# Silu taken by ScalarE's own function in two groups a tile, z kept raw and projected one tile ahead

## The chip, the cores and the metric

The kernel runs as one program on 1 core of one Trainium2 chip. The metric is the device time of that core in microseconds (us), shown as the median of several executions. The engines are called PE (TensorE, the matmuls), ACT (ScalarE), DVE (VectorE), POOL (GpSimd) and SP (SyncE, which here only issues DMAs). They run in parallel, each works off its own list of instructions in order, and they wait for each other through semaphores.

## The reference, cut to what matters

64 images of 37 tokens (36 patches and a class token) and 256 features go through an embedding, a state-space mixer, a layer norm, a mixture of experts (32 experts, 8 chosen for a row, and one shared expert) and a second layer norm. All values are float32. `_silu(v)` is `v * sigmoid(v)`. It stands in four places:

```python
x_d, z = jnp.split(xz, 2, axis=-1)
...
x_d = _silu(jnp.moveaxis(xc + conv_b[None, :, None], 1, 2))
...
delta = jax.nn.softplus(dt_raw * W_dt[:, 0] + b_dt)
...
h = dA * h + d_t[..., None] * b_t[:, None, :] * u_t[..., None]
y = jnp.einsum('bds,bs->bd', h, c_t)
...
y = jnp.moveaxis(ys, 0, 1) + D_param * x_d
y = y * _silu(z)
...
h = jax.nn.silu(flat @ wg.T) * (flat @ wu.T)
...
shared = jax.nn.silu(flat @ shared_gate_w.T) * (flat @ shared_up_w.T) @ shared_down_w.T
```

The recurrence over `h` has 16 states for each of 512 inner features, and softplus needs a logarithm and an exponential.

## The kernel before, in words

**Tiles and slots.** The images are cut into 11 tiles, the first of 4 images (148 columns) and ten of 6 (222 columns). The 512 inner features lie on 128 partitions in 4 pieces, so a full buffer of a tile is 128x888 and half of one 128x444. The first part of the program is one loop over tiles `i` and 16 slots `s`; slot `s` is also the state of the recurrence, and `g = 16 * i + s`. Every engine runs this loop by itself, in an order that the code writes out. While tile `i` does its recurrence, the slots also carry the front of tile `n = i + 1` (embedding, projection, convolution, silu, softplus) and the back of tile `t = i - 1` (gate, output projection, norm, router, shared expert), which `pieces(i, s)` of each engine places.

**One state of the recurrence.** ACT makes the decay factors, four activations for a state (`decays`, L1118: two for each of the PSUM banks D0 and D1). PE spreads the rows of B and C over the partitions into the bank BC (`spread`, L824); the bank for one state may be written once the read of the state two before is done. ACT copies B to SBUF (`copy_b`, L1106). POOL multiplies it with `du`, which is the drive (`drives`, L630), two states ahead; the drive of slot 0 is made by DVE itself (L1395). DVE scans both halves (`scan`, L1408, twice) and multiplies with C (`reads`, L1420). PE adds up the reads over the states (`add_up`, L842). A bank D can be filled for the next state only when the scan has used it.

**POOL's other work.** From tile 2 on POOL issues 16 scatters a tile (L618, rows of the tile two before, to DRAM). It also holds the expert allocation of the tile (L570 to L607, small operations in slots 12, 14 and 15), the norm's root (L413 to L418), and in slot 14 one product for softplus (L637, 128x888). DVE needs that product for `delta` (L1382) and then makes `du` (L1387), and the next tile's decays and drives need those.

**Silu before.** Silu is computed as x * (1 + tanh(x / 2)), with a factor of one half moved into later operations. ACT evaluates tanh from the PSUM bank and DVE finishes with one operation: for the convolution in slots 1 and 8 of ACT (L1056) and slots 2 and 9 of DVE (L1354), for z in slots 12 and 14 of ACT (L1062) and 13 and 15 of DVE (L1426), and for the shared expert from slot 7 (L1158, L1462).
**After the loop** follow the experts: 179 blocks of 128 rows. For each block PE turns the rows (L1001), multiplies with gate and up (L1007), turns the hidden values (L1013) and multiplies with the down weights (L1021), each step one block behind the one before it. POOL gathers the results and DVE adds them up.

## Time and profile before

| what | us |
|---|---|
| median of 3 runs | 1134.51 |
| lowest, highest | 1130.51, 1134.89 |
| the profiled execution | 1135.04 |
| its span in the trace | 1133.2 |
| DVE busy | 928.9 |
| PE busy | 964.0 |
| POOL busy | 788.1 |
| ACT busy | 681.6 |

The span is the time from the first to the last instruction in the trace; 1.8 us of the profiled execution lie around it. Busy times are sums over the whole span, and the parts have different limits: up to about 94 us the first tiles are filled in, up to about 772 us the loop over tiles runs, and from about 819 us the experts. A row of a timeline gives the start in us from the span's start, the length in us, the engine and the line of the kernel; in square brackets stands how long the engine was idle before it and what ended that.

### The profile page before, as it was taken

The page shows a single profiled execution, that of the slowest core. Times are in us where ns is not written, and L with a number is a line of the kernel's source. Part 1 is how long each engine was busy: PE and PEld are TensorE (multiplying, and loading weights), DVE is VectorE, ACT ScalarE, POOL GpSimd, SP SyncE. Part 2 cuts the span into 40 slices and gives each one's busy share as a digit, 9 for nine tenths or more (in the row PEclk, how much of TensorE's full clock was granted, in tenths as well). Part 3 has the DMA queues.
Part 4 walks back from the last instruction along what each step waited for, and adds up shares of the span by engine and source line. Part 5 has one row for each costly group of instructions (what it writes and reads, how often), then busy time and mean ns, then how long its engine had stood idle before and what let it go on. Part 6 is the DMA issues. An engine that isn't in the chain of part 4 may idle for free.

```text
span 1133.2 us, 16674 instructions
## 1 busy us (share of the span) xinstructions
PE 964.0 (85%) x4563; PEld 725.6 (64%) x4563; DVE 928.9 (82%) x1821; ACT 681.6 (60%) x1802; POOL 788.1 (70%) x839
## 2 busy tenths in 40 slices
PE   5698889988798888989978896866599999999990
PEld 5575666656566566666756663534388888878880
DVE  3589999999999999999999999896244677767774
ACT  3685675757567575666757657541266666666661
POOL 2244478878788787888878888787501676767775
PEclk8999999999999999999999999878799999999996
DMA  4599500201111020111202010058566898889883
GB/s 150 176 327 325 160 24 24 62 15 59 38 50 52 19 80 18 54 42 33 74 15 59 10 53 29 28 210 354 146 188 179 251 269 263 260 259 277 265 265 108
DMA packets 104474, 149.21 MB, mean 132 GB/s; under 512 B 14111, under 2 KB 91359, under 8 KB 104127
## 3 DMA queue, kind: packets, MB, share of 16 engines
q1 hardware_dynamic: 87487, 106.35, 29.3%
q0 software_dynamic: 16896, 41.80, 13.0%
q8 instruction: 38, 0.62, 0.2%
q14 instruction: 53, 0.43, 0.1%
HBM read 71.28 MB, written 76.82 MB: 131 GB/s over the span
## 4 chain that ended last, share of the span: by engine, by line
POOL 26%; PE 26%; issue 18%; DVE 17%; ACT 7%; DMA 3%; SPq 1%; POOLq 0%; DVEq 0%; ACTq 0%
POOL arena L630 11%; PE BC L1007 11%; DVE arena L1408 9%; POOL pool_dram L618 6%; PE Y L1001 3%; PE F L1021 3%; PE K L1021 3%; DMA mixer_own<-pool_dram 3%; DVE arena L1420 2%; ACT D L1118 2%; PE Y L842 2%; POOL arena L637 1%; PE D L1013 1%; ACT arena L1069 1%; POOL gat L686 1%
## 5 line engine op out<-in xcount | busy, mean ns | idle before, releaser
L1408 DVE TENSOR_TENSOR_SCAN arena<-D,arena 128x444 f32<-128x444 f32 (+1 forms) x352 | 351.1, 1037 | 12.4 <-ACT D L1118 8.3
L842 PE MATMUL Y<-arena,ident 128*128 128x444 f32 (+1 forms) x704 | 303.3, 559 | 1.6 <-DVE arena L1420 1.6
L686 POOL DMA_INDIRECT gat<-y_dram,slot_all x176 | 173.5, 986 | 127.5 <-DMA y_dram<-mixer_own 72.5
L618 POOL DMA_INDIRECT pool_dram<-hrow,slot_of x176 | 175.4, 997 | 45.3 <-issue 38.1
L630 POOL TENSOR_TENSOR arena<-mixer_own,arena 128x888 f32<-128x888 f32 (+1 forms) x90 | 163.9, 1823 | 53.2 <-ACT arena L1106 51.6
L1118 ACT ACTIVATE D<-mixer_own,aneg 128x216 f32<-128x216 f32 (+1 forms) x384 | 148.5, 427 | 82.4 <-DVE arena L1408 82.2
L1420 DVE TENSOR_TENSOR arena<-arena,BC 128x888 f32<-128x888 f32 (+1 forms) x176 | 184.8, 1050 | 5.4
L1007 PE MATMUL BC<-arena,xt 128*128 x716 | 185.3, 382 | 0.0
L630 POOL TENSOR_TENSOR arena<-arena 128x888 f32<-128x888 f32 x75 | 143.4, 1913 | 53.8 <-ACT arena L1106 52.9
L842 PEld LDWEIGHTS Y<-arena,ident 128*128 128x128 f32 x704 | 127.0, 199 | 74.8 <-issue 70.0
L1118 ACT ACTIVATE D<-arena,aneg 128x216 f32<-128x216 f32 x320 | 126.8, 437 | 73.1 <-DVE arena L1408 73.1
L1672 DVE SCALAR_TENSOR_TENSOR act_g<-tanh_g,BC 128x128 f32<-128x128 f32 x179 | 51.5, 288 | 106.4 <-ACT tanh_g L1259 103.9
L824 PE MATMUL BC<-bc_rows,sel 96*128 96x222 bf16 (+1 forms) x352 | 62.8, 260 | 85.9 <-DVE arena L1420 85.9
L1007 PEld LDWEIGHTS BC<-arena,xt 128*128 128x128 f32 x716 | 123.0, 192 | 9.5 <-issue 0.3
L824 PEld LDWEIGHTS BC<-bc_rows,sel 96*128 96x128 bf16 x352 | 29.4, 98 | 122.2 <-DVE arena L1420 109.5
L1106 ACT ACTIVATE arena<-BC 128x222 f32<-128x222 f32 (+1 forms) x165 | 56.4, 342 | 57.7 <-PE BC L824 57.7
L765 PEld LDWEIGHTS F<-arena 128*128 128x128 f32 x352 | 68.2, 208 | 22.0 <-issue 13.0
L1001 PE MATMUL Y<-ident,mixer_own 128*128 128x128 f32 x358 | 70.0, 278 | 11.2 <-DMA mixer_own<-pool_dram 10.8
L765 PE MATMUL F<-arena 128*128 128x210 f32 (+7 forms) x352 | 76.0, 364 | 4.0 <-DVE arena L1322 1.9
L1255 ACT ACTIVATE xt<-Y 128x256 f32<-128x256 f32 x179 | 67.2, 376 | 18.3 <-PE Y L1001 18.3
L1259 ACT ACTIVATE tanh_g<-BC 128x128 f32<-128x128 f32 x179 | 49.5, 277 | 43.1 <-PE BC L1007 43.1
L735 PE MATMUL F<-arena 128*128 128x216 f32 (+1 forms) x264 | 54.8, 364 | 21.8 <-ACT mixer_own L1070 8.7
(232 smaller groups left out, 1644.1 us busy)
## 6 DMA issues: line engine op xcount, KB each, us to landing
mixer_own<-pool_dram SPq DMA_DIRECT2D x179, 144.0 KB, 3.6
y_dram<-mixer_own SPq DMA_DIRECT2D x179, 128.0 KB
...
```

The lines of the kernel that those rows point to most:

```text
L618: nc.gpsimd.indirect_dma_start(out=pool_rows, out_offset=bass.IndirectOffsetOnAxis(ap=slot_of[q][0:r, b, k:k + 1], axis=0), in_=hrow[q][0: ...
L630: nc.gpsimd.tensor_tensor(cut(drive[g % DRIVES], i), cut(du[i % 2], i), b_row[pooled(g) % B_ROWS][:, None, 0:width(i)].broadcast_to([P, KI ...
L686: nc.gpsimd.indirect_dma_start(out=gat[0:r, k, b, :], out_offset=None, in_=y_rows[0:(blocks_by(t) - k) * P, :], in_offset=bass.IndirectOff ...
L765: nc.tensor.matmul(to.rearrange("p (a t) -> p a t", t=TOKENS)[:, :, back:], diag_w[:, c, TAPS - 1 - back, :], of[:, :, 0:TOKENS - back], s ...
L824: mm = nc.tensor.matmul(BC[g % 2][:, j * N:j * N + w], sel[:, STATES * j + s, :], bc_rows[i % 2][:, 0:w], start=True, stop=True)
L842: mm = nc.tensor.matmul(Y[j][:, 0:w], ident[:], read[g % 3][:, j * w:(j + 1) * w], start=(s == 0), stop=(s == STATES - 1), skip_group_chec ...
L1001: mm = nc.tensor.transpose(PX[b % 2][:, k * P:(k + 1) * P], xg[b % XG][:, k * P:(k + 1) * P], ident[:])
L1007: mm = nc.tensor.matmul(PG[b % 2][:, 0:DM], xt[b % 2][:, k * P:(k + 1) * P], weights[k], start=(k == 0), stop=(k == KM - 1))
L1021: nc.tensor.matmul(PY[b % 2][:, 0:DM], hidt[b % 2][:], weights, start=True, stop=True).then_inc(down_done, 1)
L1118: last = nc.scalar.activation(D[b][:, c * w:(c + 1) * w].rearrange("p (a t) -> p a t", t=TOKENS)[:, :, 1:TOKENS], cut(delta[i % 2], i)[:, ...
L1408: nc.vector.tensor_tensor_scan(state[g % 2][:, lo:hi], D[b][:, 0:hi - lo], drive[g % DRIVES][:, lo:hi], 0.0, ALU.mult, ALU.add).then_inc(s ...
L1420: nc.vector.tensor_tensor(cut(read[g % 3], i), cut(state[g % 2], i), BC[g % 2][:, None, N:N + width(i)].broadcast_to([P, KI, width(i)]), A ...
```

## The change

- ACT evaluates `Silu` itself in place of tanh, and DVE's finishing operations are gone. The factors of one half go too.
- `Silu` is in a set of its own, apart from Exp and Ln. The calls are therefore put in two groups a tile. Slot 1 holds the first half of the convolution. Slot 8 holds the shared expert's gate, the second half of the convolution and z. Behind each group the set with Exp and Ln is loaded again.
- z of tile n is projected in slots 12 and 14 of the tile before it (`project_z(n, b)` in place of `project_z(i, b)`), copied raw to SBUF by two ACT copies (`take_z`), and its silu is one operation from SBUF to SBUF (`silu_z`, 128x888) in slot 8 of the tile's own loop.
- DVE's `softplus_small` goes from slot 13 to 12, and `softplus_large` from behind the read of slot 13 to ahead of it. The shared expert's product goes from slot 8 to slot 9, between scan and read.
- In the experts, `hidden` has one DVE operation in place of two.

```diff
+            def silu_first(n):
+
+                act.wait_ge(conv_done, KI * n + 2)
+                if n > 1:
+                    act.wait_ge(x_added, n - 1)
+                    act.wait_ge(du_done, n - 1)
+                nc.scalar.activation(cut(x2[n % 2], n)[:, 0:2, :], pair(F, n), ACT.Silu).then_inc(x2_done, 1)
+                nc.scalar.preload_act_table_set("natural_log_exp_and_others")
+
+            def silu_second(n):
+                act.wait_ge(conv_done, KI * n + 4)
+                nc.scalar.activation(cut(x2[n % 2], n)[:, 2:4, :], pair(F, n), ACT.Silu).then_inc(x2_done, 1)
+
+            def take_z(n, b):
+                act.wait_ge(z_done, 2 * n + b + 1)
                 if n > 0:
...
+                    act.wait_ge(z2_done, n)
+                nc.scalar.activation(cut(z_raw, n)[:, 2 * b:2 * b + 2, :], pair(K, n), ACT.Copy).then_inc(z_taken, 1)
+
+            def silu_z(i):
+                act.wait_ge(z_taken, 2 * i + 2)
                 if i > 0:
...
+                    act.wait_ge(gated_done, 2 * i)
+                nc.scalar.activation(cut(z2, i), cut(z_raw, i), ACT.Silu).then_inc(z2_done, 1)
...
                 if front and s == 1:
-                    tanh_conv(n, 0)
+                    silu_first(n)
...
-                if back and s == (7 if mix else 9):
+                if back and s == (8 if mix else 9):
                     shared_gate(t)
                 if front and s == 8:
-                    tanh_conv(n, 1)
+                    silu_second(n)
+                if mix and s == 8:
+                    silu_z(i)
+                if mix and s == 8:
+                    nc.scalar.preload_act_table_set("natural_log_exp_and_others")
...
-                if mix and s in (12, 14):
-                    tanh_gate(i, (s - 12) // 2)
+                if front and s == 14:
+                    take_z(n, 1)
...
-                    nc.scalar.preload_act_table_set("natural_log_exp_and_others")
                     softplus_ln(n)
                     softplus_series(n)
+                    take_z(n, 0)
...
-                if front and s == 2:
-                    silu_conv(n, 0)
...
-                if front and s == 9:
-                    silu_conv(n, 1)
-                if back and mix and s == 8:
-                    shared_expert(t)
...
-                if mix and s in (13, 15):
-                    silu_z(i, (s - 13) // 2)
-                if front and s == 13:
-                    softplus_large(n)
...
+                    if 1 <= i < TILES and s == 9:
+                        shared_expert(i - 1)
                     if i + 1 < TILES and s == 12:
                         split(i + 1, 1)
+                        softplus_small(i + 1)
                     if i + 1 < TILES and s == 13:
-                        softplus_small(i + 1)
+                        softplus_large(i + 1)
...
             def hidden(b):
-                dve.wait_ge(g_tanh, b + 1)
-                nc.vector.scalar_tensor_tensor(act_g[b % 2][:], tanh_g[b % 2][:], 1.0, PG[b % 2][:, 0:HID], ALU.add,
-                                               ALU.mult).then_inc(g_act, 1)
...
+                dve.wait_ge(g_silu, b + 1)
+                nc.vector.tensor_tensor(hid[b % 2][:], silu_g[b % 2][:], PG[b % 2][:, HID:2 * HID], ALU.mult).then_inc(hid_done, 1)
```

ACT from slot 7 to slot 9 of tile 2, before. `ex` is the router's exponential, `D0` and `D1` take the decays, `BC` to arena is `copy_b`, `arena<-F` is the tanh of the convolution:

```order
L1149 ACTIVATE ex<-K 111x64
L1152 ACTIVATE ex<-ex,one_col 111x64
L1158 ACTIVATE tanh_s<-K 128x222
L1106 ACTIVATE arena<-BC1 128x222
L1118 ACTIVATE D0<-mixer_own,aneg 128x6x36 x2
L1118 ACTIVATE D1<-mixer_own,aneg 128x6x36 x2
L1056 ACTIVATE arena<-F 128x444
L1106 ACTIVATE arena<-BC0 128x222
L1118 ACTIVATE D0<-mixer_own,aneg 128x6x36 x2
L1118 ACTIVATE D1<-mixer_own,aneg 128x6x36 x2
```

The same stretch now, where L1119 is `copy_b` and L1131 the decays:

```order
L1162 ACTIVATE ex<-K 111x64
L1165 ACTIVATE ex<-ex,one_col 111x64
L1119 ACTIVATE arena<-BC1 128x222
L1131 ACTIVATE D0<-mixer_own,aneg 128x6x36 x2
L1131 ACTIVATE D1<-mixer_own,aneg 128x6x36 x2
L1171 ACT_TABLE_LOAD
L1171 ACTIVATE silu_s<-K 128x222
L1061 ACTIVATE arena<-F 128x444
L1073 ACTIVATE mixer_own<-mixer_own 128x888
L1224 ACT_TABLE_LOAD
L1119 ACTIVATE arena<-BC0 128x222
L1131 ACTIVATE D0<-mixer_own,aneg 128x6x36 x2
L1131 ACTIVATE D1<-mixer_own,aneg 128x6x36 x2
```

Between the decays of slot 8 and the `copy_b` of slot 9 stood one activation; now two table loads and three activations stand there.

ACT in slots 1 and 2 of tile 3, before and then now:

```order
L1179 ACTIVATE slot_all<-slot8 111x16
L1056 ACTIVATE arena<-F 128x444
L1118 ACTIVATE D0<-arena,aneg 128x6x36 x2
L1106 ACTIVATE arena<-BC1 128x222
L1118 ACTIVATE D1<-arena,aneg 128x6x36 x2
```

```order
L1192 ACTIVATE slot_all<-slot8 111x16
L1056 ACT_TABLE_LOAD
L1056 ACTIVATE arena<-F 128x444
L1057 ACT_TABLE_LOAD
L1131 ACTIVATE D0<-arena,aneg 128x6x36 x2
L1119 ACTIVATE arena<-BC1 128x222
L1131 ACTIVATE D1<-arena,aneg 128x6x36 x2
```

One table load stands ahead of the activation on F and one behind it, before the decays and the `copy_b` of slot 2.

DVE in slots 12 and 13, before. The first row is the pair of scans of slot 12, L1371 is `softplus_small`, L1426 the finishing of z, L1376 `softplus_large`:

```order
L1408 SCALAR_TENSOR_TENSOR arena<-D,arena 128x444 x2
L1366 TENSOR_TENSOR bc_rows<-rest,mid 32x222
L1420 TENSOR_TENSOR arena<-arena,BC 128x888
L1408 SCALAR_TENSOR_TENSOR arena<-D,arena 128x444 x2
L1371 TENSOR_SCALAR arena<-arena 128x888
L1420 TENSOR_TENSOR arena<-arena,BC 128x888
L1426 SCALAR_TENSOR_TENSOR mixer_own<-mixer_own,K 128x444
L1376 SCALAR_TENSOR_TENSOR arena<-arena,ln_small,mixer_own 128x888
```

And now, where L1418 is the scan and L1430 the read:

```order
L1418 SCALAR_TENSOR_TENSOR arena<-D,arena 128x444 x2
L1376 TENSOR_TENSOR bc_rows<-rest,mid 32x222
L1381 TENSOR_SCALAR arena<-arena 128x888
L1430 TENSOR_TENSOR arena<-arena,BC 128x888
L1418 SCALAR_TENSOR_TENSOR arena<-D,arena 128x444 x2
L1386 SCALAR_TENSOR_TENSOR arena<-arena,ln_small,mixer_own 128x888
L1430 TENSOR_TENSOR arena<-arena,BC 128x888
```

The finishing of z is gone, and the two softplus operations each stand ahead of a read.

## Rows read from the trace of the kernel before

**Rows 1.** Windows: core, busy us of each engine (instructions), TensorE's granted clock, DMA share, GB/s.
```profile
300.00:720.00 420.00, 362.01 (x1588) 257.90 (x1587) 405.44 (x583) 269.29 (x691) 347.07 (x358) 0.96 0.13 40
819.00:1100.00 281.00, 278.69 (x1526) 232.42 (x1527) 186.09 (x637) 179.75 (x524) 162.89 (x167) 1.00 0.84 248
```

**Rows 2.** Waits of DVE, 300 to 720 us: who, for whom, us, times, longest.
```profile
DVE arena L1408 <- POOL arena L630: 1.6, 6, 0.3
```

**Rows 3.** Waits of POOL, 100 to 720 us.
```profile
POOL arena L630 <- ACT arena L1106: 73.6, 63, 6.4
```

**Rows 4.** Groups of instructions on DVE: count, busy us, mean ns, idle before them.
```profile
L1672 DVE SCALAR_TENSOR_TENSOR act_g<-tanh_g,BC 128x128 f32<-128x128 f32 x179 | 51.5, 288 | 106.4 <-ACT tanh_g L1259 103.9 <-issue 1.0
...
L1354 DVE SCALAR_TENSOR_TENSOR arena<-arena,F 128x444 f32<-128x444 f32 (+1 forms) x22 | 13.1, 597 | 8.8 <-ACT arena L1056 8.8
L1426 DVE SCALAR_TENSOR_TENSOR mixer_own<-mixer_own,K 128x444 f32<-128x444 f32 (+1 forms) x22 | 13.1, 596 | 0.0
...
L1462 DVE SCALAR_TENSOR_TENSOR act_s<-tanh_s,K 128x222 f32<-128x222 f32 (+1 forms) x11 | 4.1, 373 | 0.0
```

**Rows 5.** Timeline of POOL: softplus products of tiles 1, 5, 6 and 9.
```profile
149.68 2.06 POOL L637 TENSOR_TENSOR arena<-arena 128x888 f32<-128x888 f32 x1 [1.08 <-DVE arena L1376]
...
424.92 2.08 POOL L637 TENSOR_TENSOR arena<-arena 128x888 f32<-128x888 f32 x1
...
492.87 2.09 POOL L637 TENSOR_TENSOR arena<-arena 128x888 f32<-128x888 f32 x1
...
696.94 2.08 POOL L637 TENSOR_TENSOR arena<-arena 128x888 f32<-128x888 f32 x1
```

**Rows 6.** Timeline of ACT: a table load and its neighbour, then a softplus exponential.
```profile
427.64 1.28 ACT L1062 ACT_TABLE_LOAD   x1
428.94 0.54 ACT L1062 ACTIVATE mixer_own<-K 128x444 f32<-128x444 f32 x1
...
482.72 0.94 ACT L1090 ACTIVATE arena<-arena 128x888 f32<-128x888 f32 x1
```

**Rows 7.** Timeline of POOL, tile 6: drives 4, 5, 11, 13 and 14.
```profile
444.10 1.91 POOL L630 TENSOR_TENSOR arena<-mixer_own,arena 128x888 f32<-128x888 f32 x1 [1.51 <-ACT arena L1106]
...
447.73 1.93 POOL L630 TENSOR_TENSOR arena<-mixer_own,arena 128x888 f32<-128x888 f32 x1 [0.50 <-ACT arena L1106]
...
469.03 1.92 POOL L630 TENSOR_TENSOR arena<-mixer_own,arena 128x888 f32<-128x888 f32 x1
...
479.38 1.93 POOL L630 TENSOR_TENSOR arena<-mixer_own,arena 128x888 f32<-128x888 f32 x1 [0.49 <-ACT arena L1106]
...
483.99 1.92 POOL L630 TENSOR_TENSOR arena<-mixer_own,arena 128x888 f32<-128x888 f32 x1 [0.31 <-ACT arena L1106]
```

**Rows 8.** Timeline of ACT, tile 6, slots 8 and 9: decays, then `copy_b`.
```profile
464.55 1.53 ACT L1118 ACTIVATE D<-mixer_own,aneg 128x216 f32<-128x216 f32 x4
...
467.19 0.35 ACT L1106 ACTIVATE arena<-BC 128x222 f32<-128x222 f32 x1
```

**Rows 9.** Timelines of DVE and POOL: operations beside one of the other engine.
```profile
467.78 0.17 DVE L1505 TENSOR_SCALAR gmask<-gleft 111x16 f32<-111x16 f32 x1
...
489.22 2.80 DVE L1376 SCALAR_TENSOR_TENSOR arena<-arena,ln_small 128x888 f32<-128x888 f32 x1 [0.36 <-ACT arena L1098]
...
491.23 1.63 POOL L618 DMA_INDIRECT pool_dram<-hrow,slot_of  x1 [0.17 <-issue]
...
742.13 1.91 POOL L630 TENSOR_TENSOR arena<-mixer_own,arena 128x888 f32<-128x888 f32 x1
...
742.52 1.56 DVE L1505 TENSOR_SCALAR gmask<-gleft 111x16 f32<-111x16 f32 x1
```

**Rows 10.** Timeline of DVE, tile 6: the router's weights (slot 10), then `delta` (slot 14).
```profile
476.66 0.28 DVE L1522 SCALAR_TENSOR_TENSOR wsel<-eleft,masked 111x64 f32<-111x64 f32 x1
...
495.76 1.14 DVE L1382 SCALAR_TENSOR_TENSOR arena<-arena,ln_small 128x888 f32<-128x888 f32 x1
```

**Rows 11.** The chain that ended last, fill-in of tile 0: start, us, what.
```profile
45.72 0.69 ACT D L1118 x2
```

108 lines of the change are left out of this document (41 added, 67 removed).

## The prediction

> **What bounds the kernel now.** I read the windows first, then the waits, then the timelines of one steady tile. The experts are PE's: in a window of 281.0 us PE is busy for 278.7 at a granted clock of 1.00, DVE for 186.1 [rows 1]. What DVE saves there gives nothing as long as PE stays full.
>
> The loop over tiles looks like DVE's, with 405.4 busy us of 420.0 [rows 1], and in that stretch its scans wait for POOL for only 1.6 us in all [rows 2]. But POOL is close behind. It issues sixteen scatters in each of tiles 2 to 9, and its idle time there is nearly all waits for `copy_b` on ACT [rows 3], in the slots from 1 to 4 and then in crumbs [rows 7]. A tile closes into a circle: POOL's softplus product (slot 14) ends, DVE makes `delta`, runs slots 15, 0 and 1, ACT copies B, POOL makes drive after drive and scatter after scatter up to the next product. The product starts at 149.68 in tile 1 and at 696.94 in tile 9 [rows 5], eight tiles later: 547.26 / 8 = 68.41 us a tile. In tile 6 the product ends at 492.87 + 2.09 = 494.96, and DVE takes it at 495.76 [rows 5, 10]. So POOL is only 0.8 us ahead of DVE in that circle. This is the number on which the forecast turns: DVE can come forward by 0.8 us and then waits for the product.
>
> **The change part by part.** DVE loses, for a tile, two finishing operations of the convolution and two of z at 0.60 each and one of 0.37 [rows 4]. Their overlap with the next operation is some 0.07, so they hold the queue for 4 x 0.53 + 0.3 = 2.4. The wait of 0.36 for the logarithm [rows 9] goes as well, since a table load no longer stands ahead of Ln. That is 2.8 us a tile off DVE. The product with the shared expert's up values stays, as do gate and `du`, with the same sizes.
>
> ACT gets four table loads a tile for two. A load takes 1.28, and the activation behind it starts 0.02 after its end: 427.64 + 1.28 = 428.92, then 428.94 [rows 6]. So I take 1.3 for a load with its surroundings.
>
> The Trainium skill, page "ScalarE: Activation LUTs", section "What ACT_TABLE_LOAD costs", says that a switch costs a drain of about 1.38 us beside the load. By that rule each group, with its two switches, would hold ACT for some 2.8 us more, which is an estimate from that page. The trace does not agree: no such gap stands behind the load.
>
> Slot 1: load 1.28, silu in the 0.54 of tanh (same shape, PSUM to SBUF), load 1.28: ACT is held for 3.1 us where it was held for 0.5. Queued behind are the decays of slot 3 and `copy_b` of drive 4. Slot 8: load 1.28, shared gate 0.3, convolution 0.5, z as one 128x888 operation at the 0.94 of the softplus exponential [rows 6], load 1.28: 4.3 less overlaps, 4.2. Queued behind are `copy_b` of drive 11 and the decays of slot 10. Silu itself is in no row; its bounds are those of other functions of its shape, here 0.94 for Exp, and I take no difference, since tanh, Copy and Exp of like shape lie together. The copies of raw z stand where tanh of z stood and cost the same. PE's projection of z moves one tile ahead but stays in slots 12 and 14 and waits for less; I cost it at 0 (bounds 0 and +0.5), PE's idle time in slots 10 to 15 hides it.
>
> Now the walk through tile 6, from the product's end in tile 5, 424.92 + 2.08 = 427.0. DVE starts `delta` 0.8 earlier than before, and without z's finishing in slot 15 it is 1.4 ahead at slot 1. ACT finishes the decays of slot 2 near 441.1 (worked out along the queue, as the other times without a row here) and is held until 444.2. The decays of slot 3 and `copy_b` follow, so that drive 4 starts at 445.3 and not at 444.10 [rows 7]: 1.2 late on POOL. The waits that stood before drives 5 and 10, 0.50 and 0.5, take this up. DVE too gives back most of its lead at slot 3. In slot 8 the decays end at 464.55 + 1.53 = 466.1 [rows 8], with everything as before; the block ends near 470.2, and `copy_b` at 470.5, where it started at 467.19 [rows 8]. Drive 11 starts at 470.5 in place of 469.03: 1.5 late. The waits before drives 13 and 14, 0.49 and 0.31 [rows 7], take up 0.8 of it, and behind them POOL has no wait up to the product. It ends 0.7 late, and the circle is 67.95 + 0.7 = 68.65 us (67.95 is 492.87 - 424.92), 0.25 over the mean of 68.41.
>
> That is without the second effect. In the trace DVE and POOL stop each other in some operations. `softplus_large` took 2.80 beside a drive that ended at 491.06 (0.17 before 491.23), and the scatter behind that took 1.63 [rows 9]. The router's `gmask` took 0.17 in one tile and 1.56 in another, where a drive ran from 742.13 to 744.04 and gmask ended at 744.08 [rows 9]. The page "SBUF — State Buffer" of the Trainium skill, section "SBUF: two separate sides", calls this an exclusive lock for the whole instruction; by that rule, the trace agrees.
>
> So it matters where the router's small operations meet the drives. Before, `wsel` starts at 476.66 [rows 10], just when drive 12 has ended, and takes 0.28. With drives 11 and 12 later by 1.5 and DVE 1 us early, `masked`, `wsel` and one of the softplus operations each fall into a drive: 1.5 to 1.9 us for each that does. DVE has 2 us of slack by then, the rest goes into ACT's block of slot 10, and by that into drives 13 to 15. Walked through with these stops the circle is near 70.8, 2.4 over the mean. I can't place them to half a us, so I take the middle of 0.25 and 2.4, which is 1.4 a tile. Below, a tile could gain 1.6 (2.8 less the 1.2 of slot 1, were POOL not in the way); above, I bound it by +3.0.
>
> The sum:
> - Fill-in. Two hops over DVE go (-1.0). On ACT, Exp and the first decays each need a load that they didn't need (+2.6); the decays stand on the chain [rows 11]. +1.6.
> - Tile 0 has 148 columns and no POOL limit. The blocks of slots 1 and 8 stand against shorter states, and I take +1.2 and +2.0 of their 3.1 and 4.2 as seen; the load ahead of Ln (-1.3) and one finishing of z (-0.4) go. +1.5 (0 to +4).
> - Tile 1, no scatters: -2.8 + 1.2 = -1.6.
> - Tiles 2 to 9: 8 x 1.4 = +11.2 (-13 to +24).
> - Tile 10: no front, one finishing of z and the shared one go, -0.9.
> - Experts: PE full, 0; the last block's hidden values come 0.3 sooner to the last gathers, -0.3.
>
> Together +11.5. From the profiled execution, 1135.04 + 11.5 = 1146.5; it lies 0.5 over the median of 1134.51, so I say 1146.
>
> **The rivals.**
> - DVE's relief counts. For it speaks its busy share of 97% [rows 1]. Against it stands the 0.8 us to the product. It would be -1.6 in each of eight tiles, with the rest of the sum at +0.3: 1135 - 13 = 1122. It decides if POOL has slack that I don't see, for instance if drive 11 isn't held by the block of slot 8. With the blocks hidden as well it would be 8 x -2.8, 1112.
> - POOL bounds, but the stops fall kindly: 8 x 0.25 = 2, 1137, no change.
> - A switch of tables to silu's set costs twice its row. Then slot 8 holds drive 11 for 2 x 1.28 = 2.6 more: 1146 + 8 x 2.6 = 1167. The loads of this trace speak against it, so 4 in 100. The Trainium skill's section on ACT_TABLE_LOAD, named above, is on this rival's side.
> - The change doesn't do what it says. The order shows the four loads a tile where they are meant, so I give this nothing.
>
> **How the numbers follow.** Forecast (stops and blocks lengthen tiles 2 to 9) 51, POOL bound without stops 23, relief of DVE 22, dearer switch 4 in 100. What a measurement can tell from no change is 0.5%, 5.7 us, so from 1128.8 to 1140.2. The first and the last case are slower, the second is the same, the third faster: 0.22, 0.23, 0.55. The likeliest case has 1140 to 1160 of its own. The range that leaves out 2 in 10 reaches into the first rival to 1124 and up to 1160.
>
> **What would show it.** Right: POOL's products 69 to 71 us apart in tiles 2 to 9; DVE's `delta` starting right at the product's end, with a wait; drive 11 released by `copy_b` straight behind a table load; `wsel`, `masked` or a softplus operation of 1.5 us or more; DVE's busy time in the loop down by 25 us but its waits up by more; the experts at the same time for a block. Wrong: products 67 us apart or less, DVE still without waits. Then POOL was not the limit that I read in it.

## The result and the profile after

| | before | after |
|---|---|---|
| median us (4 runs each, same chip) | 1134.7 | 1163.18 |
| lowest to highest | 1130.51 to 1137.91 | 1155.31 to 1170.39 |
| profiled execution | 1135.04 | 1168.13 |
| DVE busy | 928.9 | 888.0 |
| ACT busy | 681.6 | 724.6 |

The change makes the kernel 2.5% slower: the ratio is 1.0252, with a 95% interval of 1.0165 to 1.0338. So it is slower, while a slowdown of 2% or more is likely and not certain. Ratios, here and below, are of fast executions alone, which leaves out one of e3 (1492.69 us, with a granted clock of 0.643) and one of e2 (1277.43 us). I had forecast +11.5 us. The median moved by 28.5 and the profiled execution by 33.1. Below, line numbers of after are those of the changed kernel: scan L1418, read L1430, `softplus_small` L1381, `softplus_large` L1386, `delta` L1392, `wsel` L1523, `chosen` L1519, `masked` L1508, `gmask` L1506, drive L625, product L632, `copy_b` L1119, decays L1131.

First, where in the program does the time lie? I cut both traces at POOL's softplus products of tiles 1 and 9 [rows 5]. The windows give core, busy us of each engine (instructions), TensorE's granted clock, DMA share and GB/s. Before:

```profile
0.00:149.70 149.70, 117.79 (x574) 93.21 (x575) 112.25 (x199) 93.50 (x229) 61.25 (x76) 0.94 0.68 216
149.70:696.90 547.20, 479.31 (x2137) 344.81 (x2135) 527.64 (x762) 354.53 (x908) 454.04 (x472) 0.97 0.14 41
696.90:1133.20 436.30, 366.93 (x1854) 287.53 (x1854) 288.98 (x862) 233.57 (x666) 272.77 (x293) 0.92 0.70 216
```

After:

```profile
0.00:158.30 158.30, 125.38 (x588) 99.94 (x589) 109.30 (x191) 105.72 (x243) 61.70 (x76) 0.91 0.61 204
158.30:729.40 571.10, 486.62 (x2125) 344.80 (x2123) 541.65 (x719) 382.35 (x929) 454.27 (x473) 0.95 0.13 40
729.40:1166.30 436.90, 367.85 (x1852) 287.47 (x1852) 237.07 (x680) 236.55 (x667) 272.27 (x292) 0.93 0.69 216
```

The part up to tile 1's product is 8.6 us longer, the eight tiles are 23.9 longer, and everything behind, experts included, 0.6. The experts lost 52 us of DVE work (289.0 to 237.1) and gained nothing. In the eight tiles DVE lost work too, and yet its busy time rose by 14 us. So the second question is which of its operations grew. These are groups of DVE in the eight tiles: count, busy us, mean ns, idle us before them with what ended it. Before:

```profile
L1408 DVE TENSOR_TENSOR_SCAN arena<-D,arena 128x444 f32<-128x444 f32 x257 | 263.4, 1064 | 5.0 <-ACT D L1118 2.4 <-POOL arena L630 1.9
...
L1371 DVE TENSOR_SCALAR arena<-arena 128x888 f32<-128x888 f32 x8 | 4.8, 597 | 0.0
L1522 DVE SCALAR_TENSOR_TENSOR wsel<-eleft,masked 111x64 f32<-111x64 f32 x8 | 3.1, 382 | 0.0
L1518 DVE TENSOR_SCALAR chosen<-eleft 111x64 f32<-111x64 f32 x8 | 1.6, 195 | 0.3
```

After:

```profile
L1418 DVE TENSOR_TENSOR_SCAN arena<-D,arena 128x444 f32<-128x444 f32 x256 | 262.5, 1064 | 17.9 <-ACT D L1131 16.0 <-POOL arena L625 1.6
L1381 DVE TENSOR_SCALAR arena<-arena 128x888 f32<-128x888 f32 x8 | 20.6, 2581 | 0.2
L1523 DVE SCALAR_TENSOR_TENSOR wsel<-eleft,masked 111x64 f32<-111x64 f32 x8 | 15.9, 1986 | 0.0
...
L1519 DVE TENSOR_SCALAR chosen<-eleft 111x64 f32<-111x64 f32 x8 | 9.5, 1183 | 0.3
```

Three operations of unchanged size take several times as long: `softplus_small` 597 to 2581 ns, `wsel` 382 to 1986, `chosen` 195 to 1183. That is 1.98 + 1.60 + 0.99 = 4.6 us a tile. The scans' waits for the decays go from 2.4 to 16.0 us, 1.7 a tile. Against it stand the removed operations, 2.4 us for z and the convolution and 0.4 for the shared expert [rows 4], and 0.3 of a wait for the logarithm [rows 9]. The sum is 4.6 + 1.7 - 2.8 - 0.3 = 3.2. Measured are 3.0: the products are (729.4 - 158.3) / 8 = 71.4 us apart, where they were 68.4.

The 16.0 us of waits are of two kinds. A scan behind the block of slot 1 waits 0.90 us in each of the eight tiles. A second one, some 5 us later, waits 1.2 to 1.3 us in seven of them, and that one goes back to TensorE. Rows of tile 6, first PE (the adding up of reads, which stands ahead of the spread of B), then ACT (`copy_b`, which waits for that spread, with the decays behind it), then DVE (the scans):

```profile
460.55 5.96 PE L837 MATMUL Y<-arena,ident 128*128 128x444 f32 x8
```

```profile
468.47 0.36 ACT L1119 ACTIVATE arena<-BC 128x222 f32<-128x222 f32 x1 [2.42 <-PE BC L819]
```

```profile
464.13 2.06 DVE L1418 TENSOR_TENSOR_SCAN arena<-D,arena 128x444 f32<-128x444 f32 x2 [0.90 <-ACT D L1131]
469.56 1.08 DVE L1418 TENSOR_TENSOR_SCAN arena<-D,arena 128x444 f32<-128x444 f32 x1 [1.27 <-ACT D L1131]
```

The same eight matmuls in the same tile of e5, which is the same program executed again:

```profile
459.48 3.16 PE L837 MATMUL Y<-arena,ident 128*128 128x444 f32 x8
```

Windows over them, of after and then of e5; the granted clock is the number behind the busy times:

```profile
460.50:466.50 6.00, 6.00 (x11) 2.89 (x10) 5.03 (x6) 5.33 (x10) 1.91 (x1) 0.53 0.01 4
```

```profile
459.50:462.70 3.20, 3.20 (x12) 1.69 (x11) 2.77 (x3) 3.16 (x4) 0.00 (x0) 1.00 0.02 5
```

In e5 the second wait occurs in no tile: its scans wait 7.2 us in all, 8 x 0.90. So of the 1.7 us a tile 0.9 belong to the block of slot 1 and 1.1 to a stretch in which PE was granted half its clock, less the 0.3 of such waits that before has. The second part need not come with the program; what calls it up is open.

Why the three operations grew is seen when the two timelines of tile 6 are laid side by side. POOL:

```profile
491.22 1.91 POOL L625 TENSOR_TENSOR arena<-mixer_own,arena 128x888 f32<-128x888 f32 x1 [1.50 <-ACT arena L1119]
...
496.76 1.92 POOL L625 TENSOR_TENSOR arena<-mixer_own,arena 128x888 f32<-128x888 f32 x1
...
505.41 1.91 POOL L625 TENSOR_TENSOR arena<-mixer_own,arena 128x888 f32<-128x888 f32 x1
```

DVE:

```profile
491.93 1.25 DVE L1519 TENSOR_SCALAR chosen<-eleft 111x64 f32<-111x64 f32 x1
...
496.77 2.00 DVE L1523 SCALAR_TENSOR_TENSOR wsel<-eleft,masked 111x64 f32<-111x64 f32 x1
...
505.21 2.60 DVE L1381 TENSOR_SCALAR arena<-arena 128x888 f32<-128x888 f32 x1
```

`chosen` ends at 493.18, 0.05 after drive 11 (493.13). `wsel` ends at 498.77, 0.09 after drive 12 (498.68). `softplus_small` ends at 507.81, 0.49 after drive 14 (507.32), nearly its own length. Each stands still until the drive is over. The reads on DVE, which have one operand in PSUM, keep their 1.08 us beside the same drives. Not every operation within SBUF is stopped: just before `chosen`, a MATCH_REPLACE8 on the same tensors takes 0.18 us beside drive 11, as it does without a drive.

### The profile page after: what moved, and what is told of

Same layout as the page of the kernel before. It is cut to its first block, busy times and chain, and to the rows that moved or that the text cites. A ratio compares the mean times of both kernels' runs of the same rounds, so it can differ in the third digit from the quotient of the medians.

```text
span 1166.3 us, 16478 instructions
## 1 busy us (share of the span) xinstructions
PE 979.9 (84%) x4563; PEld 732.2 (63%) x4563; DVE 888.0 (76%) x1587; ACT 724.6 (62%) x1838; POOL 788.2 (68%) x839
## 4 chain that ended last, share of the span: by engine, by line
DVE 31%; PE 26%; issue 21%; POOL 12%; DMA 4%; ACT 4%; SPq 2%; DVEq 0%; POOLq 0%; ACTq 0%
DVE arena L1418 15%; PE BC L1005 10%; POOL arena L625 6%; DVE arena L1430 4%; POOL pool_dram L613 3%; DMA mixer_own<-pool_dram 3%; PE Y L999 3%; PE K L1019 3%; PE F L1019 2%; PE Y L837 2%; DVE arena L1381 2%; DVE wsel L1523 1%; PE F L730 1%; PE D L1011 1%; PE F L760 1%
## 5 line engine op out<-in xcount | busy, mean ns | idle before, releaser
L1418 DVE TENSOR_TENSOR_SCAN arena<-D,arena 128x444 f32<-128x444 f32 (+1 forms) x352 | 351.3, 1036 | 34.4 <-ACT D L1131 30.9
L837 PE MATMUL Y<-arena,ident 128*128 128x444 f32 (+1 forms) x704 | 312.5, 573 | 2.6 <-DVE arena L1430 2.6
L625 POOL TENSOR_TENSOR arena<-mixer_own,arena 128x888 f32<-128x888 f32 (+1 forms) x90 | 163.7, 1820 | 73.3 <-ACT arena L1119 72.2
L625 POOL TENSOR_TENSOR arena<-arena 128x888 f32<-128x888 f32 x75 | 144.5, 1927 | 67.2 <-ACT arena L1119 66.3
L1430 DVE TENSOR_TENSOR arena<-arena,BC 128x888 f32<-128x888 f32 (+1 forms) x176 | 184.6, 1049 | 4.7
L1131 ACT ACTIVATE D<-mixer_own,aneg 128x216 f32<-128x216 f32 (+1 forms) x384 | 148.5, 426 | 59.0 <-DVE arena L1418 58.6
L837 PEld LDWEIGHTS Y<-arena,ident 128*128 128x128 f32 x704 | 132.0, 207 | 81.1 <-issue 74.6
L1666 DVE TENSOR_TENSOR hid<-silu_g,BC 128x128 f32<-128x128 f32 x179 | 51.5, 288 | 163.4 <-ACT silu_g L1276 162.1
L1131 ACT ACTIVATE D<-arena,aneg 128x216 f32<-128x216 f32 x320 | 126.8, 436 | 50.3 <-DVE arena L1418 49.9
L1119 ACT ACTIVATE arena<-BC 128x222 f32<-128x222 f32 (+1 forms) x165 | 56.3, 341 | 92.5 <-PE BC L819 92.3
L760 PEld LDWEIGHTS F<-arena 128*128 128x128 f32 x352 | 67.5, 205 | 17.5 <-issue 14.6
L1276 ACT ACTIVATE silu_g<-BC 128x128 f32<-128x128 f32 x179 | 49.5, 277 | 43.9 <-PE BC L1005 43.6
```

The source lines that it names most:

```text
L625: nc.gpsimd.tensor_tensor(cut(drive[g % DRIVES], i), cut(du[i % 2], i), b_row[pooled(g) % B_ROWS][:, None, 0:width(i)].broadcast_to([P, KI ...
L760: nc.tensor.matmul(to.rearrange("p (a t) -> p a t", t=TOKENS)[:, :, back:], diag_w[:, c, TAPS - 1 - back, :], of[:, :, 0:TOKENS - back], s ...
L837: mm = nc.tensor.matmul(Y[j][:, 0:w], ident[:], read[g % 3][:, j * w:(j + 1) * w], start=(s == 0), stop=(s == STATES - 1), skip_group_chec ...
L1131: last = nc.scalar.activation(D[b][:, c * w:(c + 1) * w].rearrange("p (a t) -> p a t", t=TOKENS)[:, :, 1:TOKENS], cut(delta[i % 2], i)[:, ...
L1418: nc.vector.tensor_tensor_scan(state[g % 2][:, lo:hi], D[b][:, 0:hi - lo], drive[g % DRIVES][:, lo:hi], 0.0, ALU.mult, ALU.add).then_inc(s ...
L1430: nc.vector.tensor_tensor(cut(read[g % 3], i), cut(state[g % 2], i), BC[g % 2][:, None, N:N + width(i)].broadcast_to([P, KI, width(i)]), A ...
```

## The experiments

They ran in three groups of four, each beside before on the same chip. The second group's chip is like that of the first profiles: 432 to 437 us lie behind the last product, at 216 to 218 GB/s. On the chip of the first and third groups that part takes 548 to 565 us, at 167 to 172 GB/s, so that before itself takes 1253 and 1260 us there (the expectations name rates of windows that reach past the end of the span, 158 GB/s, which are too low). That part differs there by more than the edits explain, so small ratios of those groups prove little. Ratios are always to runs of before on the same chip. "Tile" is the distance of POOL's products of tiles 1 and 9 in the variant's own trace, over 8; this can be compared over all chips, but not without care: PE's granted clock enters into it. The same program took 71.4 us a tile in the first profile of after and 70.2 in e5, and the waits behind a halved clock (8.8 us over the eight tiles) make up nearly all of the 9.3 us between them. I give each difference against after, and where it matters the one against e5.

| run | median us | before | ratio (95%) | tile us |
|---|---|---|---|---|
| before / after, first profiles | | | 1.0252 | 68.4 / 71.4 |
| e1_small_slot13 | 1265.37 | 1253.13 | 1.0087 (1.0052 to 1.0123) | 69.4 |
| e2_slot1_copy | 1267.23 | 1253.13 | 1.0104 (1.0057 to 1.0150) | 69.9 |
| e3_slot8_copy | 1248.94 | 1253.13 | 0.9957 (0.9919 to 0.9994) | 67.9 |
| e4_scatter_moved | 1259.36 | 1253.13 | 1.0052 (1.0011 to 1.0094) | 68.6 |
| e5_after_again | 1158.50 | 1135.18 | 1.0202 (1.0167 to 1.0238) | 70.2 |
| e6_product_first | 1130.75 | 1135.18 | 0.9959 (0.9935 to 0.9984) | 67.2 |
| e7_silu_slot0 | 1133.12 | 1135.18 | 0.9981 (0.9962 to 1.0000) | 67.8 |
| e8_all | 1120.69 | 1135.18 | 0.9875 (0.9850 to 0.9900) | 66.6 |
| e9_before_scatters | 1260.73 | 1259.57 | 1.0011 (0.9989 to 1.0033) | 68.0 |
| e10_before_loads | 1277.24 | 1259.57 | 1.0149 (1.0105 to 1.0193) | 69.7 |
| e11_fill | 1245.75 | 1259.57 | 0.9885 (0.9846 to 0.9924) | 67.3 |
| e12_all_gmask | 1231.09 | 1259.57 | 0.9773 (0.9731 to 0.9815) | 65.2 |

### e1_small_slot13

```diff
                         split(i + 1, 1)
-                        softplus_small(i + 1)
                     if i + 1 < TILES and s == 13:
+                        softplus_small(i + 1)
                         softplus_large(i + 1)
```

> The kernel after, with VectorE's softplus_small issued in slot 13, behind that slot's scans, where it stood before, and no longer in slot 12 behind split. Theory A (VectorE paces the tile, and an operation of it whose operands all lie in SBUF stands still while a drive of GpSimd runs): softplus_small falls from 2.58 us to about 0.6 us in the steady tiles, the product-to-product distance falls from 71.4 to about 69.4 us, and the time by 16 us, to about 1147 us; the same edit takes 2 us off tile 1. If softplus_large thereby starts behind drive 15 of GpSimd and no longer beside it, up to 1.9 us a tile more goes. Theory B (the tile is paced by the chain copy_b, drive, product on ScalarE and GpSimd, and VectorE's stops fill time in which it would wait anyway): softplus_small gets short all the same, but as much idle time appears on VectorE ahead of a scan, and the time stays within 3 us of 1163.

Groups of DVE from 158 to 729 us, which are the eight tiles and the start of a ninth:

```profile
L1523 DVE SCALAR_TENSOR_TENSOR wsel<-eleft,masked 111x64 f32<-111x64 f32 x8 | 14.7, 1841 | 0.0
...
L1392 DVE SCALAR_TENSOR_TENSOR mixer_own<-arena,ln_small 128x888 f32<-128x888 f32 x5 | 5.7, 1142 | 7.6 <-POOL arena L632 7.6
L1381 DVE TENSOR_SCALAR arena<-arena 128x888 f32<-128x888 f32 x8 | 4.8, 596 | 0.0
```

`softplus_small` is back at 596 ns, and `softplus_large` came free as well (1143 ns for 2830). 3.7 us of stops went, but the tile shortened by 2.0 only, since `delta` now waits for the product, up to 1.9 us each time. Theory A holds in its number against after; against e5's 70.2 the tile gained 0.9. What it had not said is that the next limit lies so close.

### e2_slot1_copy and e3_slot8_copy

```diff
-                nc.scalar.activation(cut(x2[n % 2], n)[:, 0:2, :], pair(F, n), ACT.Silu).then_inc(x2_done, 1)
-                nc.scalar.preload_act_table_set("natural_log_exp_and_others")
+                nc.scalar.activation(cut(x2[n % 2], n)[:, 0:2, :], pair(F, n), ACT.Copy).then_inc(x2_done, 1)
```

e3 does the same to `silu_second`, `silu_z` and `shared_gate`, and drops the load behind them. Both leave out the silu of what they copy, so they measure time alone.

> The kernel after, with the slot-1 group's silu replaced by a plain copy and the table load behind it left out: silu of half the convolved channels is not computed, everything else is. ScalarE's block in slot 1 shrinks from 3.1 to 0.54 us. Theory A (this block makes VectorE's scans wait, 0.90 and 1.27 us in the trace of after): the waits of scans for decays fall from 2.0 us a tile to under 0.4, the distance from product to product falls by about 2 us, the time by 16 us for the eight steady tiles and by 3 to 5 more in the fill-in, to 1142 to 1145 us. Theory B (the scan's second wait is due to TensorE's spread of B and not to the block, and the first is made up for later in the tile): under 5 us off, 1158 to 1163.

> The kernel after, with the three silu of the slot-8 group (second half of the convolution, gate of the shared expert, z) replaced by plain copies and the two table loads around them left out. The block of 4.2 us shrinks to 1.9. No scan of the steady tiles waits there, so the wait of VectorE for ScalarE stays. Theory A (the block's harm is that drive 11 of GpSimd starts 1.5 us late, and so beside chosen, and drive 12 beside wsel): chosen falls from 1.18 to about 0.2 us, wsel perhaps from 2.0 to 0.4, and the tile gets 1 to 2.6 us shorter: 1142 to 1155 us. Theory B (ScalarE has the time for it and the stops of chosen and wsel come from elsewhere): no change, 1160 to 1166.

Without the block of slot 1 the scans' waits for decays are 4.8 us in eight tiles, for 16.0, and the tile is 1.5 shorter; `softplus_small`, `wsel` and `chosen` stay as long as in after. So this block costs a wait and is not what brings the stops. The wait of 0.90 is gone from every tile. What is left, 4.8 us, is a wait of 0.7 to 1.0 in five tiles, each with a stretch of halved clock on PE just ahead; so theory B was right on the second wait. The forecast was 2 us a tile. Against after 1.5 came, but against e5 0.3 (69.9 for 70.2), and no more than the 0.9 of the first wait can be put down to the block. The rest of its gain lay ahead of tile 2, whose first read came 7.3 us earlier (162.3 for 169.65). Some 4 us of that are again the clock's and not the edit's, as e11 shows; the 3.4 that are left against e4 are within the 3 to 5 that I expected.

Without the block of slot 8 the tile loses 3.4 us, though no scan had waited there. From the groups of DVE in the eight tiles (here `wsel` is L1521, `softplus_small` L1379, `chosen` L1517):

```profile
L1506 DVE TENSOR_TENSOR masked<-score,gmask 111x64 f32<-111x64 f32 x8 | 8.4, 1056 | 0.0
...
L1521 DVE SCALAR_TENSOR_TENSOR wsel<-eleft,masked 111x64 f32<-111x64 f32 x8 | 5.4, 669 | 0.0
L1379 DVE TENSOR_SCALAR arena<-arena 128x888 f32<-128x888 f32 x8 | 5.0, 623 | 0.3
...
L1517 DVE TENSOR_SCALAR chosen<-eleft 111x64 f32<-111x64 f32 x8 | 1.6, 196 | 0.3
```

All three are free or nearly so, and `softplus_large` as well (1.2 us for 2.83): more than theory A asked for. In their place `masked` meets a drive (1.06 us for 0.22). The second wait is still there in five tiles. Against e5 the tile loses 2.3 us. The block's price was paid on another engine: `copy_b` behind it was late, POOL's drives 11 to 15 with it, and DVE ran into them.

### e4_scatter_moved

```diff
-SCATTERS = (0, 0, 1, 1, 1, 0, 1, 1, 2, 3, 2, 2, 1, 1, 0, 0)
+SCATTERS = (0, 0, 1, 1, 1, 1, 1, 1, 2, 2, 2, 2, 1, 1, 0, 0)
```

> The kernel after, with one of the three scatters of slot 9 issued in slot 5, where there was none. Nothing is left out. Drive 12 of GpSimd then starts about 1.27 us earlier, at 495.5 where it was 496.76, and VectorE's wsel, which begins at 496.77, meets only its last 0.6 us. Theory A (wsel stands still for what is left of the drive beside it): wsel falls from 1.99 to about 1.0 us or less, the time by 8 to 11 us, 1152 to 1155; softplus_small, beside drive 14, gets shorter too if drive 14 is also earlier. Theory B (what VectorE does not lose there it loses at the next meeting): the sum of chosen, wsel, softplus_small and softplus_large stays at 8.6 us a tile and the time at 1163.

Groups of DVE in the eight tiles:

```profile
L1508 DVE TENSOR_TENSOR masked<-score,gmask 111x64 f32<-111x64 f32 x8 | 11.6, 1444 | 0.0
L1506 DVE TENSOR_SCALAR gmask<-gleft 111x16 f32<-111x16 f32 x8 | 8.0, 999 | 0.3
...
L1381 DVE TENSOR_SCALAR arena<-arena 128x888 f32<-128x888 f32 x8 | 5.0, 624 | 0.3
...
L1523 DVE SCALAR_TENSOR_TENSOR wsel<-eleft,masked 111x64 f32<-111x64 f32 x8 | 1.8, 219 | 0.0
```

One scatter in another slot, with all work and all table loads in place, makes the tile 2.8 us shorter than in after and 1.6 shorter than in e5; the scans' waits for decays, 9.5 us for 16.0, are 0.8 of the 2.8. Neither theory had it right. `wsel` is wholly free, and with it `softplus_small`, `softplus_large` and `chosen`, but `gmask` and `masked` are stopped now (2.0 us together). The sum of those four fell from 8.6 to 2.2 us, and by what theory B said it should have stayed. The tile is at 68.6, and `delta` waits 1.14 us for the product in the tile shown:

```profile
431.77 1.14 DVE L1392 SCALAR_TENSOR_TENSOR mixer_own<-arena,ln_small 128x888 f32<-128x888 f32 x1 [1.14 <-POOL arena L632]
```

The prediction had walked through a circle without stops, bound by the product, at 68.65. The number is the same, but a scatter stands elsewhere here and two operations are stopped, so this is no test of that walk.

How `softplus_small` came free is worth a look. DVE's row, then POOL's drive 14, in one tile of e4:

```profile
420.63 0.62 DVE L1381 TENSOR_SCALAR arena<-arena 128x888 f32<-128x888 f32 x1
```

```profile
420.83 2.19 POOL L625 TENSOR_TENSOR arena<-arena 128x888 f32<-128x888 f32 x1 [0.32 <-issue]
```

DVE's row starts 0.20 us ahead of the drive's, as it does in after (505.21 against 505.41). There DVE was held for 2.60 us and the drive kept its 1.91; here DVE keeps its 0.62 and it is the drive that takes longer.

### e5_after_again

> The kernel after, unchanged, beside the three variants of this group, because the chip that ran the first group moved the experts' data more slowly (158 GB/s where the profiles of before and after had 216) and its times stand about 115 us above the others. Its mixer should read as in the first profile of after: product to product 71.4 us, softplus_small 2.58, wsel 1.99, chosen 1.18 us, last product 729 us. If the phase in which VectorE's operations meet GpSimd's drives is a matter of chance from run to run, these numbers come out differently, for instance 68.5 us; if it is set by the order of the program, they repeat within 0.3 us.

Neither: the tile took 70.2 us on average, single ones between 69.4 and 70.8. Groups of DVE in a window of the same length (here over eight to nine tiles):

```profile
L1381 DVE TENSOR_SCALAR arena<-arena 128x888 f32<-128x888 f32 x8 | 18.7, 2339 | 0.3
L1523 DVE SCALAR_TENSOR_TENSOR wsel<-eleft,masked 111x64 f32<-111x64 f32 x8 | 14.7, 1832 | 0.0
...
L1392 DVE SCALAR_TENSOR_TENSOR mixer_own<-arena,ln_small 128x888 f32<-128x888 f32 x5 | 6.0, 1198 | 2.4 <-POOL arena L632 2.4
```

The stops are there as in after in seven of the eight tiles; only the last has others (`masked` 1.85 us, `wsel` 0.70, `softplus_small` 0.62), and that lowers the means. What is missing is the second wait: 7.2 us of waits for decays where after had 16.0. These 8.8 us are nearly the 9.3 by which the eight tiles are shorter, and go back to PE's clock, as shown above. The two profiled executions, 1168.13 and 1156.60, lie 11.5 apart. That the same thing makes after's wide spread (15 us in four executions, where before has 7) is likely and not shown, since only profiled executions have a trace.

### e6_product_first, e7_silu_slot0 and e8_all

e6, against after:

```diff
-SCATTERS = (0, 0, 1, 1, 1, 0, 1, 1, 2, 3, 2, 2, 1, 1, 0, 0)
+SCATTERS = (0, 0, 1, 1, 1, 1, 1, 1, 2, 2, 2, 2, 1, 0, 1, 0)
```

e7 has e4's scatters and this; e8 has e6's scatters, this, and the second piece:

```diff
-                if front and s == 1:
+                if front and s == 0:
                     silu_first(n)
...
-                if mix and s == 8:
+                if (front or mix) and s == 8:
                     nc.scalar.preload_act_table_set("natural_log_exp_and_others")
```

> The kernel with one scatter moved from slot 9 to slot 5 (68.47 us a tile), and with the scatter of slot 13 moved behind the softplus product of slot 14. Nothing is left out. Theory A (once VectorE's stops are gone, GpSimd's product bounds the tile: VectorE's delta waited 1.3 us for it there, with no wait for it in the kernel after): the product starts 1.1 us earlier, delta's wait goes, and the tile takes 67.3 to 67.6 us; the last product about 8 us earlier than with the scatter alone (703 to 695) and the time 8 us lower. Theory B (the tile of 68.5 is set by ScalarE's copies of B and TensorE's spread, and delta's wait only fills slack): the wait moves to the next scan, 68.3 to 68.6 us.

> The kernel with one scatter moved from slot 9 to slot 5, and with the slot-1 group of ScalarE (load, silu, load) moved to slot 0, where VectorE has its own drive, the gate and both scans and ScalarE's decays waited 2.15 us for it. Theory A (the group's harm in slot 1 is a wait of VectorE's scans, 1.2 to 2 us a tile, and slot 0 has slack for it): waits of scans for decays fall from 1.18 to under 0.5 us a tile; since GpSimd's product then bounds, the tile gains little of it: 67.8 to 68.5 us. Theory B (its copy of B for drive 3 is late now, so GpSimd's drives are late): the tile gets longer, 69 us or more. The fill-in gets 1 to 3 us shorter.

> Everything together, with nothing left out: scatter from slot 9 to 5, scatter of slot 13 behind the product, the slot-1 silu group in slot 0, and in the fill-in one table load behind the slot-8 silu in place of three behind softplus_exp, softplus_ln and the first decays. Theory A (the costs found are separate: stops on VectorE, product last, block in slot 1, three loads in the fill-in): 66.3 to 67.5 us a tile, the first read of the state 2.6 us earlier than in the kernel after, and a time below that of before by 5 to 15 us. Theory B (the tile's length is that of the phase in which VectorE and GpSimd meet, and each move deals the stops anew): 68 to 71 us a tile, and no gain over before.

In e6 POOL's product comes straight behind drive 15, with no scatter between, and `delta` then starts with no wait. POOL and DVE in one tile:

```profile
425.90 1.92 POOL L625 TENSOR_TENSOR arena<-arena 128x888 f32<-128x888 f32 x1
427.78 2.07 POOL L632 TENSOR_TENSOR arena<-arena 128x888 f32<-128x888 f32 x1
```

```profile
429.94 1.14 DVE L1392 SCALAR_TENSOR_TENSOR mixer_own<-arena,ln_small 128x888 f32<-128x888 f32 x1
```

The tile loses 1.4 us against e4. So the product did bound it there: theory A. In e7 the scans' waits for decays fell from 9.5 us to 5.7 over the eight tiles, and the tile gained 0.8. The waits for the product stayed. Here too the tiles are of two kinds, 66.7 to 67.6 us for five of them, and 69.4, 68.6 and 70.0 for the first and the last two, which have a scan's wait of 0.9, 0.8 and 2.3 behind a halved clock. e8 has the sum of it, at 66.6 us, and beats before by 14.5 us. Theory A again. Its first read came 6.0 us earlier than in after (45.78 for 51.76), where I had expected 2.6; e11 takes that apart.

### e9_before_scatters and e10_before_loads

e9 is before with e6's line of scatters. e10 is before with this:

```diff
                 if front and s == 1:
                     tanh_conv(n, 0)
+                    nc.scalar.preload_act_table_set("silu_and_others")
+                    nc.scalar.preload_act_table_set("exp_and_others")
...
                 if front and s == 8:
                     tanh_conv(n, 1)
+                    nc.scalar.preload_act_table_set("silu_and_others")
+                    nc.scalar.preload_act_table_set("exp_and_others")
```

> The kernel before, with tanh and all, and only the order of GpSimd's scatters changed as in the fastest variants: one from slot 9 to slot 5, the one of slot 13 behind the product. It tells how much of the gain over before belongs to the scatters alone. Theory A (before is bound by VectorE, which never waited for the product in its steady tiles and met two stops, softplus_large's 1.8 us and few others): 66.5 to 68.6 us a tile, of which less than 1 us is gain if the stops stay. Theory B (the scatters are the whole gain, and VectorE's relief by silu is worth nothing): 66.5 to 67 us a tile, as in the variants with silu on ScalarE.

> The kernel before, with nothing changed but two pairs of table loads added on ScalarE, one behind the first half's tanh in slot 1 and one behind the second half's in slot 8 (2.57 us each). VectorE has all its work as before. Theory A (the table loads are what costs: in slot 1 the scans wait for the decays, in slot 8 GpSimd's drive 11 is late and the meetings with VectorE's operations move): scans wait 1.5 to 2.2 us a tile more, and stops of VectorE may grow by 0 to 4 us: 70 to 72.5 us a tile, 1150 to 1175 us in all. Theory B (the stops came from softplus_small's new place and from VectorE's being earlier, not from the loads): 68.3 to 69.5 us a tile.

e9 says that the scatters alone do nothing for before (1.0011): DVE binds there and keeps its work. In the variants with silu on ACT they open the way for what DVE has saved. Between e9 and e12 the tile is 2.7 us shorter, which is nearly the 2.8 that DVE was relieved of. But e12 has another scatter moved as well, which before was never given, and fewer stretches of halved clock, so the match is in part luck.

e10 fell between its theories: 1.3 us a tile over before's 68.4, and 1.8 over e9 on the same chip. DVE's groups:

```profile
L1412 DVE TENSOR_TENSOR_SCAN arena<-D,arena 128x444 f32<-128x444 f32 x257 | 263.1, 1064 | 6.8 <-ACT D L1118 5.6 <-POOL arena L630 0.8
...
L1511 DVE TENSOR_TENSOR masked<-score,gmask 111x64 f32<-111x64 f32 x8 | 8.6, 1074 | 0.0
```

The loads add 0.4 us a tile of waits of scans and about 1.2 in stops, in `masked` and `wsel` (681 ns), but `softplus_small` and `chosen` stay free. Loads of after's length, without its other edits, thus bring 1.6 us of waits and stops a tile, where after has 6.3. That the block of slot 8 has a part in the rest is shown by e3, and `softplus_small`'s new place by e1. That DVE's being earlier has one as well is only argued.

### e11_fill

It is e6 with the second piece of e8's diff alone.

> The variant with the scatter of slot 9 in slot 5 and that of slot 13 behind the product (first read of the state at 51.95 us, tile 2's first read at 169.84), with one change: in the fill-in, ahead of tile 0, ScalarE loads the table of exp and ln right behind the slot-8 silu, so that the loads ahead of softplus_exp, softplus_ln and the first decays fall away (three for one). Theory A (those loads lie on the chain of the fill-in): first read at 49.4 us or a little more, 2.5 us earlier, and 2 to 4 us of it left at tile 2. Theory B (VectorE's split and TensorE's projections set the fill-in): no change of the first read. The tiles stay at 67.0 us.

The first read came 5.8 us earlier than in e6 (46.12 for 51.95), and 6.1 us were left at the product of tile 1 (152.30 for 158.45): more than twice theory A's number. But e6 ran on the other chip, and PE's rows show that more than the loads differs. Rows are start, length, instruction and its idle time. In after, e11 and e4:

```profile
44.23 3.33 PE L746 MATMUL F<-h,arena 128*128 128x222 f32 x8 [2.65 <-DVE h L1328]
```

```profile
41.57 1.77 PE L746 MATMUL F<-h,arena 128*128 128x222 f32 x8 [0.67 <-DVE h L1328]
```

```profile
43.76 1.77 PE L746 MATMUL F<-h,arena 128*128 128x222 f32 x8 [2.65 <-DVE h L1328]
```

These two are windows over them, of after and then of e4; the granted clock is the number behind the busy times:

```profile
44.20:47.60 3.40, 3.33 (x8) 2.52 (x8) 0.66 (x1) 0.01 (x1) 0.00 (x0) 0.50 1.08 391
```

```profile
43.70:45.60 1.90, 1.77 (x8) 1.43 (x8) 0.68 (x2) 0.03 (x1) 0.00 (x0) 1.00 1.08 390
```

The eight matmuls ran at 0.50, the level of 1.2 GHz, in after, e1, e5 and e6, and took 3.33 us. In e2, e4 and e7 they ran at 1.00 and took 1.77, and in all seven PE had stood idle for 2.65 us before them. So that wait alone does not lower the clock, and what does is open. It matters up to the product of tile 1, to which after, e4, e5 and e6 run the same program: there after and e6 need 158.3 and 158.5 us, e5 160.8, and e4 154.3.

The fair comparison for e11 is therefore e4, on the same chip and at 1.00 in these matmuls. Against it the first read is 3.6 us earlier (46.12 for 49.74), and 2.0 are left at the product of tile 1. Theory A had 2.5 and 2 to 4. Three loads of 1.28 are 3.8; the one put in their place starts at 29.49, where ACT had been waiting for PE, and so costs nothing. One of the three stood ahead of the first decays, here in after:

```profile
48.15 1.28 ACT L1131 ACT_TABLE_LOAD   x1
```

For after's first read that makes 0.8 (PE's later start than before) + 1.6 (clock) + 1.3 (load) = 3.7 us against before, which is what it was late (51.76 for 48.03). Of these the 1.6 need not come with the program.

### e12_all_gmask

```diff
-SCATTERS = (0, 0, 1, 1, 1, 1, 1, 1, 2, 2, 2, 2, 1, 0, 1, 0)
+SCATTERS = (0, 0, 1, 1, 1, 1, 1, 0, 3, 2, 2, 2, 1, 0, 1, 0)
```

> The variant with everything together (66.5 us a tile), and the scatter of slot 7 moved to slot 8, so that drive 10 of GpSimd starts 1.1 us earlier and is over when VectorE's gmask begins, and masked begins ahead of drive 11. There gmask took 1.04 and masked 1.65 us beside these drives, where alone they take 0.20 and 0.22. Theory A (a stop goes when the meeting goes): gmask about 0.2 us, masked 0.2 to 0.9 us; VectorE is up to 2.2 us earlier, then the product and the drives bound, which gain 0.5 to 1.3 us a tile: 65.2 to 66.0. Theory B (GpSimd bounds already and VectorE's gain becomes a wait for drives or the product): 66.3 to 66.8 us a tile.

Groups of DVE in the eight tiles:

```profile
L1519 DVE TENSOR_SCALAR chosen<-eleft 111x64 f32<-111x64 f32 x8 | 8.0, 1005 | 0.3
L1523 DVE SCALAR_TENSOR_TENSOR wsel<-eleft,masked 111x64 f32<-111x64 f32 x8 | 6.0, 753 | 0.0
...
L1508 DVE TENSOR_TENSOR masked<-score,gmask 111x64 f32<-111x64 f32 x8 | 1.8, 219 | 0.0
L1506 DVE TENSOR_SCALAR gmask<-gleft 111x16 f32<-111x16 f32 x8 | 1.4, 178 | 0.3
```

e8's stops of `gmask` and `masked`, 2.2 us, went, new ones of 1.3 came (`chosen`, `wsel`), and the tile is at 65.2: theory A in its tile time. Part of it is the clock again. e8's tiles take 65.6 us (the first and the seventh somewhat more) where no halved clock meets the slots from 1 to 3, and 67.3 to 67.5 where one does; six of e12's eight have none, at 64.8 or less. Like for like the scatter is worth some 0.8, an estimate from these rows. This is the fastest version, 2.3% under before. On a chip of the first kind it was not timed.

## Why the prediction was wrong

The direction was right and the size was not: +11.5 forecast, +33.1 in the profiled execution, +28.5 in the median, outside of the range. Two terms were too small, that of tiles 2 to 9 and that of the fill-in with tiles 0 and 1, and a cost that both leave out is PE at half its clock. By its steps:

- **"Tiles 2 to 9: 8 x 1.4."** This is the term that failed, with 12.7 us of the 21.6 missed. The walk with stops had come out at 70.8 a tile, 2.4 over the mean, and I halved it by taking the middle between it and a walk without stops. There was nothing to halve: the stops came in all eight tiles of after and in seven of e5's, and the eighth has others. That is some 8 us. Measured were 3.0 a tile, since in the first profile a wait behind PE's halved clock, 1.1 us a tile, came on top, which is in no term. Without it, in e5, the tile took 70.2, 1.8 over, and its longest tiles 70.8, the very number of the walk. That the sum of this walk is so near is in part luck, for its parts differ, as the next points say.
- **"So POOL is only 0.8 us ahead of DVE in that circle."** From this I let DVE wait for the product. Wrong in after: over the eight tiles `delta` never waited. The stops held DVE back by more than the relief had given. It was right as a statement on the next limit: `delta` waits for the product in e1 and e4, and e6 shows that the product bounds the tile there.
- **Which operations are stopped.** I named `masked`, `wsel` and one of the softplus operations, 1.5 to 1.9 each. They were `chosen` (1.0), `wsel` (1.6) and `softplus_small` (2.0). The cause, slot 8's block that delays `copy_b` and drive 11 by 1.5 us, stands in the trace as forecast (491.22, with its wait of 1.50), and e3 shows that without it the stops go.
- **"DVE too gives back most of its lead at slot 3."** It did: behind the block of slot 1 a scan waits 0.9 us in each tile, where I had counted 1.2 against the relief. The other 1.1 us a tile in the first profile are PE's clock.
- **Loads.** 1.28 us each, and the next activation 0.02 later: right. Silu lasts as long as tanh of its shape (0.54), and z 0.95 where I took 0.94. The drain in "What ACT_TABLE_LOAD costs" of the Trainium skill's page "ScalarE: Activation LUTs" shows in none of the 50 loads of after: behind 46 of them the next activation starts within 0.15 us, and behind the others it waits for PE. The rival built on it falls, although its time (1167) lies close to the result. That time came about otherwise.
- **Fill-in, tile 0 and tile 1: +1.5 together.** Measured +8.6, which is 7.1 of the 21.6 missed. Some 4 of the 8.6 are PE's halved clock: e4, with the same program up to there, came to tile 1's product at 154.3 us for 158.3. Without it the term is about +4.6 against before, or +3.8 against e9 on e4's chip. The rest was under-counted: three loads on the chain are worth 3.6 us at the first read, of which 2.0 are left (e11 against e4), and the block of slot 1 is worth 3.4 by tile 1's product (150.9 in e2 for 154.3 in e4).
- **Tile 10, experts and tail: -1.2.** Measured +0.6. The experts' zero was right: PE stayed full, 276.2 busy us of 280.0 from 850 us on, at a granted clock of 1.00.
- **Signs.** I had said that DVE's busy time in the loop would fall by 25 us and its waits grow by more. It rose by 14, because a stopped operation counts as busy.

Not settled is what gives PE half its clock in one execution and not in another of the same program, and how much `softplus_small`'s new place alone would cost in before; it was not tried there.
